# New orders of the work with SyncE's transfers in them, token numbers loaded in four portions, drains on GpSimd, and a later wait for the experts, in a two-layer language-model tower

## What is computed

```python
h = table[x]                                            # gather of embedding rows
h = h + attn0(layernorm(h))      # causal linear attention, elu features, 16 heads, then a layernorm
h = h + (layernorm(h) @ CB.T) * (SCB / 127) + bias
h = h + attn1(layernorm(h))      # random-feature attention, layernorm, relu MLP 256-1024-256, layernorm
x = layernorm(h)                 # last block: 8 experts, top 1, and a shared expert
moe = score * expert[argmax(x @ router.T)](x)           # each a silu-gated MLP 256-512-256
h = h + moe + (silu(x @ shared_gate) * (x @ shared_up)) @ shared_down
```

## Time and profile before

| | us |
|---|---|
| median of 3 runs (lowest, highest) | 753.63 (753.06, 753.99) |
| the profiled execution's own time | 751.52 |
| its span, first to last instruction | 749.7 |
| TensorE busy, VectorE, ScalarE, GpSimd | 676.8, 463.6, 277.2, 274.0 |
| mean granted TensorE clock | 0.967 of full speed |

### The profile page before, as it was taken

One profiled execution on the slowest core, in us unless ns is written; L12 is line 12 of the kernel. 1 busy time (PEld: TensorE's weight loads), 2 busy tenths in 40 slices (PEclk: granted clock), 3 DMA queues, 4 the chain that ended last, 5 costly groups with the idle time before them and its releaser, 6 DMA issues.

```text
span 749.7 us, 15139 instructions
## 1 busy us (share of the span) xinstructions
PE 676.8 (90%) x5738; PEld 555.5 (74%) x5739; DVE 463.6 (62%) x1148; ACT 277.2 (37%) x664; POOL 274.0 (37%) x424
## 2 busy tenths in 40 slices
PE   3899899999999999999999999999950599999993
PEld 2677788889988989888898989898840265656561
DVE  2788888888877877778777776675540022232320
ACT  1335445545435354453544444543200022222220
POOL 4252432542525434252432432422201245454531
PEclk9999999999999999999999999999986599999996
DMA  8930000000000000000000000003420211111100
GB/s 270 414 143 2 8 9 2 8 16 8 9 15 16 15 16 9 15 2 15 9 8 16 1 16 15 8 8 106 151 82 1 85 36 51 33 39 63 63 28 10
DMA packets 17296, 34.18 MB, mean 46 GB/s; under 512 B 7617, under 2 KB 12240, under 8 KB 15952
## 3 DMA queue, kind: packets, MB, share of 16 engines
q1 hardware_dynamic: 12640, 24.89, 9.3%
q0 software_dynamic: 4592, 8.41, 3.7%
HBM read 28.74 MB, written 7.29 MB: 48 GB/s over the span
## 4 chain that ended last, share of the span: by engine, by line
PE 81%; DVE 5%; DMA 3%; issue 3%; SPq 3%; ACT 2%; POOL 2%; POOLq 0%; DVEq 0%; ACTq 0%
PE ps L1067 74%; PE ps L1072 4%; PE ps L1245 2%; DMA home_rows<-send_home 2%; SPq L343 1%; SPq L344 1%; DVE S_sb L759 1%; DMA sorted_ids<-tokens,slot_u 1%; ACT qkA L672 1%; DVE stats L696 1%; ACT yTB L662 1%; POOL H L364 1%; DMA we<-w_experts 1%; POOL rstd L396 1%; PE ps L1381 0%
## 5 line engine op out<-in xcount | busy, mean ns | idle before, releaser
L1067 PE MATMUL ps<-yTC,we 128*128 128x128 f32 x1024 | 125.8, 277 | 0.0
L1067 PEld LDWEIGHTS ps<-yTC,we 128*128 128x128 f32 x1024 | 121.1, 192 | 4.7 <-issue 3.4
L395 POOL TENSOR_TENSOR var_eps<-mv,ln_eps 128x1 f32<-128x1 f32 x112 | 39.8, 356 | 176.3 <-DVE mv L697 175.9
L1067 PE MATMUL ps<-we,yTA 128*128 128x256 f32 (+1 forms) x288 | 97.1, 468 | 2.5 <-ACT yTB L662 0.9
L1067 PE MATMUL ps<-we,yTB 128*128 128x256 f32 (+1 forms) x216 | 74.1, 474 | 0.0
L1067 PEld LDWEIGHTS ps<-we,yTA 128*128 128x128 f32 x288 | 52.4, 196 | 26.9 <-issue 21.8
L396 POOL TENSOR_TENSOR rstd<-var_eps,pow_half 128x1 f32<-128x1 f32 x112 | 68.8, 615 | 8.8
L450 POOL TENSOR_TENSOR preB<-yB,rows_sb 128x256 f32<-128x256 f32 x16 | 15.2, 949 | 145.1 <-DVE mv L697 145.1
L1067 PE MATMUL ps<-we,ffT 128*128 128x256 f32 x256 | 60.8, 380 | 0.0
L1067 PEld LDWEIGHTS ps<-we,yTB 128*128 128x128 f32 x216 | 39.5, 190 | 26.8 <-issue 24.4
L1067 PEld LDWEIGHTS ps<-we,ffT 128*128 128x128 f32 x256 | 46.2, 190 | 5.0
(11 more groups left out here) (196 smaller groups left out, 1369.2 us busy)
## 6 DMA issues: line engine op xcount, KB each, us to landing
we<-w_experts SPq DMA_DIRECT2D x7, 1536.0 KB, 15.4
we<-w_ff SPq DMA_DIRECT2D x2, 1024.0 KB, 7.7
x_rows<-send_x SPq DMA_DIRECT2D x16, 128.0 KB, 1.7
home_rows<-send_home SPq DMA_DIRECT2D x16, 128.0 KB, 1.7
rows_sb<-rows SPq DMA_DIRECT2D x1, 1664.0 KB, 6.2
we<-w_experts SPq DMA_DIRECT2D x3, 512.0 KB, 4.6
we<-w_qk SPq DMA_DIRECT2D x2, 512.0 KB, 4.4
we<-w_v SPq DMA_DIRECT2D x2, 256.0 KB, 4.5
```

Source lines behind the costliest of these rows:

```text
L395: link(pool.tensor_tensor(var_eps[:, k:k + 1], mv[:, k, 1:2], ln_eps[:], ALU.add))
L1067: return pe.matmul(o, a, b, start=start, stop=stop)
```

## The change

1. All five lists have another order and other lags, SyncE's included, with PSUM banks given out anew and the `after` waits that go with that. The lags of TensorE's list now begin at 2 and end at 12 (0 and 10 before).
2. SyncE's one `load_ids` becomes four steps for 2, 2, 8 and 11 tiles, placed apart; only the first waits for the table and the scatter. GpSimd waits for a portion before the round that first needs it.
3. GpSimd executes `drain` before its first wait for token numbers and before `store` in rounds 3, 7 and 11.
4. TensorE transposes the first two tiles before it waits for the experts, no more after.
5. VectorE's `c_norm` no longer waits for `sent_ready`, `a_norm` waits for `src0T_psum`, `a_vz` for `den0_psum`, `b_norm` for `preB_ready`; GpSimd's `pB` no longer waits for `var4_ready`.

```diff
+    IDS_FROM = [0, MOE_SLOTS, 2 * MOE_SLOTS, 6 * MOE_SLOTS, SORTED_TILES]
...
-        sc = [ps[:, 0, :], ps[:, 6, :], ps[:, 4, :], ps[:, 1, :]]
-        xk = ps[:, 2:4, :]
-        xq = ps[:, 0:2, :]
-        qT = ps[:, 0:2, :]
+        sc = [ps[:, 7, :], ps[:, 6, :], ps[:, 3, :], ps[:, 5, :]]
+        xk = ps[:, 3:5, :]
+        xq = ps[:, 6:8, :]
+        qT = ps[:, 2:4, :]
...
-            def load_ids(t):
-
-                if t < T - 1:
-                    return
-                sp.wait_ge(S["table_ready"], 1)
-                sp.wait_ge(S["ids_scattered"], 16 * T)
-                for j in range(SORTED_TILES):
+            def load_ids(n):
+
+                for j in range(IDS_FROM[n], IDS_FROM[n + 1]):
                     sp.sem_inc(S["unused"], 1)
                     first = sp.value_load(tile_row[0:1, j:j + 1], min_val=0, max_val=E * SPAN * P)
                     sp.dma_start(ids[:, j:j + 1], sorted_ids[bass.ds(first, P), :]
-                                 ).then_inc(S["ids_loaded0" if j < MOE_SLOTS else "ids_loaded1"], 16)
+                                 ).then_inc(S[f"ids_loaded{n}"], 16)
+
+            def ids0(t):
+
+                if t == T - 1:
+                    sp.wait_ge(S["table_ready"], 1)
+                    sp.wait_ge(S["ids_scattered"], 16 * T)
+                    load_ids(0)
...
             run_steps([
-                (5, home_out), (3, x_out), (0, free_b), (1, free_ff), (3, free_ga), (3, load_ids), (3, free_up),
-                (4, free_dn),
+                (6, free_dn), (0, free_b), (10, ids2), (3, free_up), (0, free_ff), (4, home_out), (12, ids3),
+                (2, ids0), (5, ids1), (2, free_ga), (1, x_out),
             ])
...
-            pool.wait_ge(S["ids_loaded0"], 16 * MOE_SLOTS)
+            def ids_for(i):
+                for n in range(4):
+                    if IDS_FROM[n] == i * MOE_SLOTS:
+                        pool.wait_ge(S[f"ids_loaded{n}"], 16 * (IDS_FROM[n + 1] - IDS_FROM[n]))
+
+            pool.drain()
+            ids_for(0)
             pool.wait_ge(S["x_kept"], 16 * T)
             fetch_x(0)
-            pool.wait_ge(S["ids_loaded1"], 16 * (SORTED_TILES - MOE_SLOTS))
+            ids_for(1)
             fetch_x(1)
             pool.wait_ge(S["home_kept"], 16 * T)
             fetch_home(0)
             for i in range(ROUNDS):
                 if i + 2 < ROUNDS:
+                    ids_for(i + 2)
                     fetch_x(i + 2)
+                if i % 4 == 3:
+                    pool.drain()
                 store(i)
...
             def a_s(t):
...
-                after(pe, "qT_ready", t - 3)
-                after(pe, "src5T_ready", t - 4)
-                after(pe, "ff2_read", t - 5)
+                after(pe, "rden0_ready", t)
+                after(pe, "logit_copied", t - 6)
+                after(pe, "v0_ready", t + 1)
...
             pe.wait_ge(S["table_ready"], 2)
-            pe.wait_ge(S["experts_loaded"], 16 * (E + 1))
...
             transpose_x(0)
+            pe.wait_ge(S["experts_loaded"], 16 * (E + 1))
```

More of the change, by code:

```diff
@@ L727, in a_norm @@
             def a_norm(t):
+                after(dve, "src0T_psum", t)
                 normalise(yA[:], H[:, t, :], 0, t).then_inc(S["src0_ready"], 1)
@@ L754, in a_vz @@
                 dve.wait_ge(S["v0_psum"], t + 1)
+                after(dve, "den0_psum", t)
                 dve.tensor_tensor(parity_apart(vz[:]), by_parity(v0[:, 0:D]), by_parity(row["v0_bias"]), ALU.add
@@ L826, in b_norm @@
             def b_norm(t):
+                after(dve, "preB_ready", t)
                 normalise(yB[:], H[:, t, :], 3, t).then_inc(S["src3_ready"], 1)
@@ L1034, in _ @@
             run_steps([
[L1035 to L1040, removed]
+                (6, b_km), (11, table3), (6, b_dgr), (10, table0), (6, b_vo), (12, c_down), (7, b_rec), (6, kmx),
[4 more added lines that the diff above has]
+                (8, c_res), (10, c_gc),
             ])
@@ L1098, in a_qk @@
                 pe.wait_ge(S["src0T_ready"], t + 1)
+                after(pe, "ff2_read", t - 6)
                 by_channel(qk0, yTA, qk0_sb, range(4)).then_inc(S["qk0_psum"], 1)
@@ L1125, in a_num @@
                 pe.wait_ge(S["scores_masked"], t * 4 + 4)
+                after(pe, "src6T_ready", t - 5)
                 for half in range(2):
@@ L1150, in a_rdenT @@
                 pe.wait_ge(S["rden0_wide"], t + 1)
+                after(pe, "src3T_ready", t - 1)
                 transposed(rdenT0, rdenTA).then_inc(S["rden0T_psum"], 1)
@@ L1159, in a_T2 @@
                 pe.wait_ge(S["src2_ready"], t + 1)
-                after(pe, "counts_read", t - 4)
                 transposed(T2, yA2).then_inc(S["src2T_psum"], 1)
@@ L1173, in b_T3 @@
                 pe.wait_ge(S["src3_ready"], t + 1)
+                after(pe, "ffb_ready", (t - 3) * 4 + 4)
                 transposed(T3, yB).then_inc(S["src3T_psum"], 1)
@@ L1201, in b_dg @@
                 pe.wait_ge(S["square_ready"], t + 1)
-                after(pe, "tile_done", t - 5)
+                after(pe, "src5T_ready", t - 1)
                 for c in range(4):
@@ L1229, in b_k @@
                 pe.wait_ge(S["qk1_ready"], t * 4 + 4)
-                if t + 2 < T:
-                    after(pe, "src1T_ready", t + 3)
+                after(pe, "qT_ready", t)
+                if t + 3 < T:
+                    after(pe, "scores_masked", (t + 3) * 4 + 1)
                 features(xk, KD).then_inc(S["xk_psum"], 1)
@@ L1243, in b_qT @@
                 pe.wait_ge(S["qfeat_ready"], t + 1)
+                if t + 3 < T:
+                    after(pe, "rden0T_out", t + 4)
+                if t + 4 < T:
+                    after(pe, "scores_masked", (t + 4) * 4 + 1)
                 for pair in range(PAIRS):
@@ L1274, in b_h @@
                 pe.wait_ge(S["qT_ready"], t + 1)
+                if t + 4 < T:
+                    after(pe, "scores_masked", (t + 4) * 4 + 3)
                 for n in range(2):
@@ L1299, in c_T5 @@
                 pe.wait_ge(S["x1_ready"], t + 1)
-                if t + 2 < T:
-                    after(pe, "src3T_ready", t + 3)
+                if t + 1 < T:
+                    after(pe, "qT_ready", t + 2)
                 transposed(T5, x1).then_inc(S["src5T_psum"], 1)
@@ L1325, in c_f1 @@
                 pe.wait_ge(S["ffa_ready"], t * 4 + 4)
-                if t + 2 < T:
-                    after(pe, "kexp_in", t + 3)
+                if t + 7 < T:
+                    after(pe, "src0T_ready", t + 8)
+                after(pe, "hT_ready", t - 2)
                 second_layer(t, 0)
@@ L1335, in c_T6 @@
                 pe.wait_ge(S["src6_ready"], t + 1)
+                if t + 2 < T:
+                    after(pe, "rden1T_out", t + 3)
                 transposed(T6, yC).then_inc(S["src6T_psum"], 1)
@@ L1339, in c_lo @@
                 pe.wait_ge(S["src6T_ready"], t + 1)
+                if t + 3 < T:
+                    after(pe, "qexp_in", t + 4)
                 by_token(lo[:, 0:E], yTC2[t % AHEAD], router_sb, KD).then_inc(S["logit_psum"], 1)
@@ L1349, in c_up @@
                 pe.wait_ge(S["src6T_ready"], t + 1)
+                if t + 2 < T:
+                    after(pe, "ff2_read", t + 3)
                 by_channel(up, yTC2[t % AHEAD], su_sb, range(KE)).then_inc(S["up_psum"], 1)
@@ L1367, in _ @@
             run_steps([
-                (8, c_T6), (5, b_kmB), (2, a_num), (5, b_q), (2, a_den), (7, c_fb), (7, c_f1), (2, a_denT), (1, a_v),
-                (8, c_lo), (5, b_ctx0), (5, b_qT), (5, b_ctx1), (4, b_T3), (7, c_f2), (5, b_ctx2), (2, a_rdenT),
-                (6, c_T5), (4, b_qk), (5, b_ctx3), (10, c_dn), (1, a_s), (4, b_k), (5, b_h), (4, b_dg), (4, b_v),
-                (8, c_cn), (5, b_denT), (0, a_T0), (2, a_out), (6, c_fa), (5, b_rdenT), (3, a_T2), (0, a_qk),
-                (9, c_up), (4, b_kmT), (4, b_dgT), (3, a_ffn), (5, b_out), (8, c_ga),
+                (5, a_out), (7, b_kmT), (6, a_T2), (9, c_fa), (7, b_kmB), (8, b_rdenT), (6, a_ffn), (12, c_up),
[3 more added lines that the diff above has]
+                (7, b_h), (6, b_dg), (6, b_v), (6, b_dgT), (12, c_dn), (7, b_denT),
             ])
             pe.wait_ge(S["table_ready"], 2)
-            pe.wait_ge(S["experts_loaded"], 16 * (E + 1))
             def transpose_x(i):
```

87 lines of the change are left out of this document (42 added, 45 removed).

## The result

The changed kernel takes 729.97 us, the median of 4 runs (728.91 to 732.64), against 753.35 us for the kernel before beside it (752.61 to 753.99, 4 runs). The ratio is 0.9695, with a 95% interval of 0.9667 to 0.9724. The profiled execution took 730.55 us, with a span of 728.6.

What follows compares the result with a forecast made beforehand. TensorE bounds the full tower, with a hole behind it from SyncE's number loads and a long end drain. +6.5 - 21.9 + 0.5 + 0 - 6 = -20.9 us, from the median 753.63 to 732.7 us, range 723 to 743.

Steps and rivals of the forecast that it cites:

- What bounds the kernel: TensorE fills the tower; behind it a hole, largely SyncE's 23 number loads at 1.16 us each; GpSimd's 9.56 us DRAIN ends it.
- The portions, -21.9 us: From the last scatter's landing to the first expert matmul: 11.0 us instead of 32.9, the first rows' gather arriving last.
- The stall behind the experts, +6.5 us: Tile 11's write waits behind 3 MB of experts; the last tile's routing follows it, so the last scatter is issued later.
- F: Moment when the last tile's `c_f2` is done and SyncE may issue experts 5 and 6; 534.54 us in the profile before.
- the rival of a free write: Tile 11's write does not stand behind the experts and lands 1.7 us after issue: 720 us in all; chance 0.06.
- Round 2's numbers, +0.5: The third portion, 8 numbers for rounds 2 to 5, may make TensorE wait for round 2's rows: 0 to 2 us.
- The new orders in the tower, 0: TensorE's work per tile and depth stay the same, so no change in the tower, with bounds of -4 and +4 us.
- The drains, -6 us: Drains inside GpSimd's waits shorten the 8.3 us end drain: gain at most 7.0, some 1 us showing in the rounds.
- The reading by count: A drain's length is work gathered with GpSimd's indirect DMAs since the last drain, 8.3 us for 101 of them.
- The end did shrink: Answers the rival that the final DRAIN is fixed and the new ones hide: 739 us; chance 0.24.
- a drain does not cost a fixed 8.3 us: Answers the rival that every drain costs 8.3 us and the end keeps its own: 746 us; chance 0.07.
- The scores' wait for `v0`: Rival in the tower: `a_s` waits for VectorE's `a_vz` in every tile; 757 us at 1.5 us per tile; chance 0.05.

Runs made afterwards that it cites:

- e7_before_portions: The kernel before, its orders untouched, with token numbers loaded in four portions (2, 2, 8, 11 tiles) at later places of SyncE's list: 731.27 us, ratio 0.9706.
- e3_ids_at_once: The changed kernel with all four portions of token numbers loaded at the place of the first: 752.16 us, ratio 0.9987 to the kernel before.
- e4_wait_first: The changed kernel with TensorE's wait for the experts back ahead of the first transposes: 730.36 us, ratio 0.9692 to the kernel before.
- e10_act_queue: The changed kernel with experts 5 and 6 issued on ScalarE's queue instead of SyncE's: 722.17 us, ratio 0.9594 to the kernel before.
- e11_before_act: The kernel before, orders untouched, with portions and drains, and experts 5 and 6 issued on ScalarE's queue: 722.85 us, ratio 0.9594.
- e1_no_drains: The changed kernel without any of GpSimd's added drains: 736.29 us, ratio 0.9785 to the kernel before.
- e9_before_both: The kernel before, its orders untouched, with the portions and the drains added: 724.61 us, ratio 0.9609.
- e2_two_drains: The changed kernel with two drains only, ahead of the first wait for token numbers and in the last round: 731.56 us, ratio 0.9729 to the kernel before.
- e12_ff_later: The kernel before with portions and drains, `free_ff` moved from lag 1 to lag 2 in SyncE's list, behind two more small writes: 720.03 us, ratio 0.9566.
- e5_ff_last: The changed kernel with `free_ff` moved to the end of SyncE's list, so two tile writes go ahead of the two experts: 723.20 us, ratio 0.9603.

## Why the prediction was right

By its own steps:

- **What bounds the kernel.** Right. The hole held 22 us of SyncE's loads; `e7_before_portions` alone took them out, `e3_ids_at_once` put them back.
- **The portions, -21.9 us.** Measured -21.90 in the profiles and 21.7 by `e7_before_portions`. The gather of the first rows, not the experts, is the later of the two, as the sum had it, and `e4_wait_first` confirms that the later wait costs and gains nothing.
- **The stall behind the experts, +6.5 us.** Measured +6.80. The landing came at F + 15.6 (forecast 15.1), then `c_down` to scatter 7.8 us (8.1), with `c_ga` at 3.69 us on a cold TensorE (3.6). The reason given for the landing, a write that stands behind the same 3 MB, holds, and the rival of a free write fell. It landed 14.7 us after its issue, a little above the 12 to 14 that I had named as the sign. But I read the earlier trace rows as an order within SyncE's queue, and so did my expectations of `e10_act_queue` and `e11_before_act`; these two runs show that another queue does not free the write.
- **Round 2's numbers, +0.5.** Nothing shows: the rounds took 148.94 us against 148.86. The gather of round 2 did start late, 4.45 us after GpSimd was free, and TensorE did not wait for it.
- **The new orders in the tower, 0.** Right as far as the runs can tell. F is +1.35 in this pair, but it stands at 534.1 to 536.0 us in the seven kept traces with the new orders and at 534.5 to 537.2 in five with the old ones, so the two orders reach F at the same time within what executions differ. The difference is there early: VectorE's `a_x` of one tile starts at 205.2 in `e1_no_drains` and at 207.0 in the changed kernel, which have the same tower, with a granted clock of 1.00 and 0.94 in the first 30 us, and at 216.9 and 219.5 in the kernel before and `e9_before_both`. Within the tower two things stand against each other. A full iteration is longer, by the `a_x` of one tile in six successive iterations, first and last start (line, what, ns, start):

```profile
L734 DVE TENSOR_TENSOR xA<-ps,cols_sb x6: 691/692/692, 216.9 to 379.5; 128x512 f32<-128x512 f32 x6
```
```profile
L762 DVE TENSOR_TENSOR xA<-ps,cols_sb x6: 691/692/692, 207.0 to 371.6; 128x512 f32<-128x512 f32 x6
```

(379.5 - 216.9)/5 = 32.52 us before and (371.6 - 207.0)/5 = 32.92 after, at the same matmuls and a TensorE without an idle stretch in both. The kept traces of the other kernels show the same two lengths. Over the iterations shown that makes 2.0 us, and since F does not move, the filling and the end of the tower give about as much back, as the prediction had said of the filling. Why the new order of TensorE costs 0.4 us per iteration was not settled; no experiment took it apart.
- **The drains, -6 us.** The term of the sum that was sized low by one microsecond: -7.02, the upper end of its bounds. The last drain goes on for 1.2 us behind the store's instruction, as forecast (1.3). The reading by count gave `e2_two_drains` within 0.1 us, but not the first drain, which also waits for the scatter's landing. The drains in rounds 3 and 7 make the store 1.8 us late, more than the 1 us forecast, and the slack of the home rows takes it, as forecast. The Trainium skill (VectorE: DVE Perf Modes, The DRAIN you can't avoid) gives about 12 ns for the DRAINs that the runtime puts at a program's start and end. The prediction applied this to the end of the kernel's own block; the drain there took 9,560 ns on GpSimd, and 2,433 ns with drains ahead of it, so the page's figure is not one for it.
- **The rivals.** The end did shrink, a drain does not cost a fixed 8.3 us, the write is not free. The scores' wait for `v0` does not appear among TensorE's waits, which between 80 us and 540 us are at most 0.6 us each.

The forecast of 732.7 lay 2.7 us above the measured median. By the spans of the two profiled executions the sum was right, -20.9 against -21.1. That it came so close is in part luck: the microsecond too little for the drains and the 1.35 us by which this pair differs up to F stand against each other. The 2.7 us lie between profiles and medians: the profiled execution before, 751.52, was 2.1 below the median of 753.63 to which the sum was carried over, and the one after, 730.55, is 0.6 above its own.

## What to carry to other kernels

A serial loop of small loads ahead of one that everything waits for is worth its whole length; issue only what the first round needs. In a plan, put small transfers that others wait for ahead of a bulk load, in time and not by queue, early enough to land before it starts, and look which small transfer then falls into its shadow. If GpSimd issues many indirect DMAs, drain it in waits that it has anyway, near the end above all; and test each part of a joint change alone, as here the orders cost 5 to 7 us inside a gain of 23.

## What was not expected

- A 128 KB write issued up to 6 us behind two 1.5 MB loads took 10.5 us (`e12_ff_later`) to 16.3 us (`e3_ids_at_once`) on their queue, and 10.9 and 13.0 on another (`e11_before_act`, `e10_act_queue`); alone it takes 1.7. The Trainium skill, DMA: Bandwidth & Descriptors, Queues, rings and completion order, has each engine go round its queues by packets, and by the packet counts above `e11_before_act` agrees. By that alone the write should have been much shorter. The same section says that a transfer's completion signal lands only after every earlier write of its engine, across the queues, which would hold the write's signal back; no run here takes the two apart.
- The indirect scatter of 128 numbers is slow everywhere: 5.2 to 9.5 us in the full tower, with no expert load in flight, 6.4 to 8.3 for the last one in the other kernels, and 11.03 beside the loads in `e12_ff_later`. In `e5_ff_last` and `e10_act_queue` the last scatter was in flight beside them too and took 7.2 and 8.3 us; it was issued 10 us behind them there, and 7 us behind them in `e12_ff_later`. Why it takes so long without them was not looked into.
- Expert 4's load, 1.5 MB on SyncE's queue, lands 16.0 to 17.6 us after its issue in the seven traces with the new orders and 6.2 to 6.5 us after it in the six with the old ones. In the changed kernel the DMA engines are busy for 0.82 of the time from 525 to 530 and move only 48 GB/s. What slows it was not looked into.
- GpSimd's drain grows with every indirect DMA since the last one, by 0.04 us for each up to 32 and some 0.085 beyond, though all those DMAs but the last have landed long before.
